# When ScalarE sums and squares an input tile, and where its shift comes from, in the shift-and-sign-convolution stage of a four-layer network

## The reference

```python
x = x + _L0_conv_ref(_gn(x), W, b, 224)   # mean over pixels @ W + b -> offsets (dy, dx), clipped to 0..28; gn(x) shifted by them
x = x + _L1_conv_ref(_gn(x), W, b)        # 3x3 convolution of sign(gn(x)) with the sum of four sign kernels, + bias
x = x + _L2_conv_ref(_gn(x), ...)         # DCT x FFT, mixing of 32 x 32 modes, inverse; + pointwise layer; relu
x = x + _L3_conv_ref(_gn(x), ...)         # the same with other weights
```

## Time and profile before

| | us |
|---|---|
| median of three runs | 3744.3 |
| the profiled execution | 3783.59 |
| its span (first to last instruction) | 3781.8 |
| PE busy | 3024.4 (80%) |
| DVE busy | 2752.2 (73%) |
| ACT busy | 1478.2 (39%) |
| first stage within it, roughly | 60 to 1893 |
| bodies 1 to 13 (first `add_conv` of body 1 to that of body 14) | 273 to 1730 |

### The profile page before, as it was taken

One profiled execution on the slowest core, in us unless ns is written; L12 is line 12 of the kernel. 1 busy time (PEld: TensorE's weight loads), 2 busy tenths in 40 slices (PEclk: granted clock), 3 DMA queues, 4 the chain that ended last, 5 costly groups with the idle time before them and its releaser, 6 DMA issues. The chain is left out here.

```text
span 3781.8 us, 58575 instructions
## 1 busy us (share of the span) xinstructions
PE 3024.4 (80%) x17264; PEld 1393.2 (37%) x17264; DVE 2752.2 (73%) x3864; ACT 1478.2 (39%) x2708; POOL 36.9 (1%) x23
## 2 busy tenths in 40 slices
PE   0288888888888888889937888989898835999997
PEld 0033334333334333344425333333333315444443
DVE  3887777787778687788342767676767644899998
ACT  3466666576666566664423322222222213000000
POOL 0000000000000000000010000000000010000000
PEclk9988888798888798889966999999898866999998
DMA  4676665666656566665274564646465353999998
GB/s 145 184 224 191 200 188 179 192 203 194 191 181 195 173 200 196 204 195 172 91 137 184 230 252 183 248 179 252 188 244 203 139 124 102 342 394 385 379 384 306
DMA packets 272195, 808.65 MB, mean 214 GB/s; under 512 B 85466, under 2 KB 119774, under 8 KB 261108
## 3 DMA queue, kind: packets, MB, share of 16 engines
q1 hardware_dynamic: 212948, 488.15, 40.9%
q10 hardware_dynamic: 58368, 316.72, 21.6%
q0 software_dynamic: 608, 0.63, 0.1%
HBM read 479.39 MB, written 329.56 MB: 214 GB/s over the span
## 5 line engine op out<-in xcount | busy, mean ns | idle before, releaser
L1397 ACT ACTIVATE B_junk<-B_im,B_nk 128x896 bf16<-128x896 f32 x224 | 232.7, 1039 | 749.3 <-DVE B_im L1455 610.4
L839 DVE SCALAR_TENSOR_TENSOR A_image<-A_cps,A_cbias,A_image 128x896 f32<-128x896 f32 x224 | 257.4, 1149 | 239.5 <-PE A_cps L470 239.1
L509 PE MATMUL A_vps<-A_tout,a_k_dctj 112*32 112x512 f32 x896 | 294.6, 792 | 150.6 <-ACT A_tout L614 150.6
L470 PE MATMUL A_cps<-A_sign,A_cfull 128*128 128x448 bf16 x1344 | 404.7, 384 | 7.7 <-issue 7.7
L1648 PE MATMUL C_ring<-C_im,C_wnorm 128*128 128x448 f32 x896 | 388.1, 572 | 23.7 <-DVE C_ubuf L1705 18.3
L1315 PE MATMUL B_ring<-B_rout,iB_k_rowf 128*64 128x512 f32 x896 | 306.6, 774 | 118.4 <-DVE B_rout L1448 118.4
L1343 PE MATMUL B_ring<-B_im,B_wnorm 128*128 128x448 f32 x896 | 384.9, 571 | 7.1 <-DVE B_wnorm L1426 4.9
L1455 DVE SCALAR_TENSOR_TENSOR B_im<-B_ring,B_im 128x896 f32<-128x896 f32 x224 | 239.0, 1084 | 183.9 <-PE B_ring L1353 182.3
L475 PE MATMUL A_cps<-A_sign,A_cedge 32*32 32x448 bf16 x1344 | 363.7, 379 | 0.0
L477 PE MATMUL A_cps<-A_sign,A_cedge 32*32 32x448 bf16 x1344 | 363.4, 378 | 0.0
L614 ACT ACTIVATE A_tout<-A_aps 112x512 f32<-112x512 f32 x448 | 246.1, 589 | 288.8 <-PE A_aps L498 288.3
(11 more groups left out here) (193 smaller groups left out, 3444.6 us busy)
## 6 DMA issues: line engine op xcount, KB each, us to landing
A_rin<-in_x SPq DMA_DIRECT2D x2016, 112.0 KB, 2.4
x2s<-A_image ACTq DMA_DIRECT2D x112, 896.0 KB, 4.6
B_im<-x2s SPq DMA_DIRECT2D x112, 896.0 KB, 9.7
x3s<-B_im ACTq DMA_DIRECT2D x112, 896.0 KB
C_im<-x3s SPq DMA_DIRECT2D x112, 896.0 KB, 11.9
out<-C_rout ACTq DMA_DIRECT2D x192, 256.0 KB
out<-C_rout ACTq DMA_DIRECT2D x192, 192.0 KB
out<-C_rout ACTq DMA_DIRECT2D x64, 128.0 KB
```

The source lines that it names most:

```text
L470: return nc.tensor.matmul(banks[:, s, 0:LPN], cfull[:, tap, :], lines(n, s, slice(0, P), 0, tap), start=(tap == 0), stop=(tap == 2), skip_ ...
L509: last = nc.tensor.matmul(vps[32 * g:32 * g + 32, :], con["k_dctj"][:, half, :], tout[G % OUTS][:, half, :], start=(half == 0), stop=(half ...
```

## The change

ACT's work on an input tile moves one slot later: `stat_tiles(s)` gives the load tiles of slot s - 1, and for each both sum and square are taken, in this order, with no lag between the two. `guess` no longer reads ACT's sum: DVE reduces the first 56 elements per partition of the image (part of tile 0) right after turning tile 0, waits for its own turn and its own reduce, and scales. In slot 14 ACT's `square` of output unit 13 comes ahead of `lower`. `PER` counts DVE's chained steps per body, one more now. The number of ACT instructions, of DMAs and of matmuls is the same.

```diff
-        def x_ops(k):
-            return [("sum", k)] + [("square", j) for j in {15: (13, 14, 15)}.get(k, (k - 2,)) if j >= 0]
+        def stat_tiles(s):
+            return x_tiles(s - 1) if s else range(0)
...
-                for k in x_tiles(s) if has_x else ():
-                    for op in x_ops(k):
-                        place[op] = len(place)
+                for k in stat_tiles(s) if has_x else ():
+                    for op in ("sum", "square"):
+                        place[op, k] = len(place)
...
             def x_tile(b, q, k, tile):
                 sum_x(b, q, k, tile)
-                if k >= 2:
-                    square_x(b, q, k - 2)
-                if k == TILES - 1:
-                    square_x(b, q, k - 1)
-                    square_x(b, q, k)
+                square_x(b, q, k)
...
+                    if has_v and 1 <= s <= UNITS:
+                        square(b, q, s - 1)
                     if has_x and s == 14:
                         lower(b + 1, (q + 2) % 3)
-                    if has_v and 1 <= s <= UNITS:
-                        square(b, q, s - 1)
                     if has_v and s in (5, 9, 13):
                         copy_rows(b, (s - 5) // 4)
-                    for k in x_tiles(s) if has_x else ():
+                    for k in stat_tiles(s) if has_x else ():
                         x_tile(b + 2, (q + 2) % 3, k, tile_no(b, x_at(k)))
...
-            def guess(b):
-                dve.wait_ge(junk_done, junk_x(b, ("sum", 0)) + 1)
-                nc.vector.tensor_scalar(nx[:], xsum[:, 0:1], -1.0 / TN, None, ALU.mult).then_inc(nx_ready, 1)
+            def guess(b, q):
+                dve.wait_ge(tile_turned, 1 if isinstance(b, int) and b == 0 else tile_no(b - 2, x_at(0)) + 1)
+                link(nc.vector.tensor_reduce(sm[:, 30:31], image[q][:, 0:2 * CHQ], AX.X, ALU.add))
+                nc.vector.tensor_scalar(nx[:], sm[:, 30:31], -0.5 / CHQ, None, ALU.mult).then_inc(nx_ready, 1)
...
-                if k == 2:
-                    guess(0)
+                if k == 0:
+                    guess(0, 0)
...
-                        if k == 2:
-                            guess(b + 2)
                         if k >= 8:
                             dve.wait_ge(junk_done, junk_x(b + 2, ("square", k - 8)) + 1)
                         turn_x(far, k, x_at(k) % RING, tile_loaded(b, x_at(k)))
+                        if k == 0:
+                            guess(b + 2, far)
...
-            PER = 41
+            PER = 42
```

## The result

The change makes the kernel slower: 3811.8 us in the median of four runs (3809.8 to 3820.3) against 3746.8 for the kernel before on the same chip, a ratio of 1.0145 (95% interval 1.0091 to 1.0199). I had forecast 3745. The ratios in this text are worked out from the single runs and aren't the quotients of the medians (that is 1.0173 here, or 65 us); by the ratio the loss is some 54 us. They leave out three runs in a slow state of the chip (one each of e1, e8 and the kernel before), which the medians hold.

What follows compares the result with a forecast made beforehand. Chains with waits, no full engine, were taken to bound the first stage. Points 1 to 4 summed as 0 + 0 + 0.8 + 0 = +0.8 us on 3744.3, giving 3745 us, range 3710 to 3774.

Steps and rivals of the forecast that it cites:

- What bounds it now: First stage: no engine full; chains with waits bound it, PE pacing slots 0 to 4, then DVE and SP's queue.
- Point 1, statistics one slot later: Slots 8 to 11: `copy_back` comes earlier, PE's idle time moves behind `forward_cols`; taken as 0, at most 50 us.
- The slower rival: Slot 11: PE's idle time now ends at unit 12's conv, at half clock; 3763 us, up to 3797; chance 0.33.
- no change: Whole kernel: the likeliest case, 3745 us, own range 3737 to 3752; chance 0.36.
- the clock has its own phase: Unit 12's conv: argument against all bodies turning slow, as the clock need not follow PE's gap; no size given.
- the 3 to 5 us that I had put down: Slot 11: forecast length of PE's idle time after `turn_back`, right up to DVE's sums.
- Point 2, the weight in even slots: ACT's statistics shift from odd to even slots, hidden behind other work; slot 2's 1.94 us wait stays; taken as 0.
- Points 3 and 4, the shift and the square: Shift in slot 0: +0.8 us in all; square first starts DVE's body 1.3 to 2.5 us sooner, swallowed: 0.
- The rival in which the earlier start counts: Body start: DVE's 1.3 to 2.5 us are not swallowed in slots 3 and 4; 3712 to 3727 us; chance 0.14.

Runs made afterwards that it cites:

- e1: The changed kernel with the old order, strips ahead of the output square; 3821.7 us, ratio 1.0158 against the kernel before.
- e8: The changed kernel with 34 unused matmuls on PE in slot 11, between `turn_back` and the averages; 3768.5 us, ratio 1.0055 against the kernel before.
- e7: The changed kernel with the first six stores of the output image issued one slot later; 3804.7 us, ratio 1.0161 against the kernel before.
- e10: The changed kernel with 28 unused matmuls on PE in slot 9, behind `forward_cols`; 3832.7 us, ratio 1.0153 against the kernel before.
- e2: The kernel before with only the output square put ahead of the strips; 3755.2 us, ratio 0.9998 against the kernel before.
- e3: The kernel before with only the shift taken from DVE's reduce behind the first turn; 3775.7 us, ratio 1.0040 against the kernel before.
- e9: The kernel before with 20 unused matmuls on PE ahead of slot 11's `forward_cols`; 3762.1 us, ratio 0.9987 against the kernel before.

## Why the prediction was wrong

*What bounds it now* held, but for a slip: 1451 us isn't the whole of bodies 1 to 13 (it is 1456.7, or 112.1 us a body instead of 111.6). DVE waits as before in slots 3 and 4; the rows of body 8 that answer to the earlier trace rows:

```profile
1124.14 1.15 DVE L836 SCALAR_TENSOR_TENSOR A_image<-A_cps,A_cbias,A_image 128x896 f32<-128x896 f32 x1 [4.22 <-PE A_cps L470]
...
1135.47 1.15 DVE L836 SCALAR_TENSOR_TENSOR A_image<-A_cps,A_cbias,A_image 128x896 f32<-128x896 f32 x1 [3.84 <-PE A_cps L470]
```

*Point 1, statistics one slot later: the step that failed.* Its 0 was wrong in two places, at the convs of units 12 and 13 (some 33 us with the slots behind them) and in the slots of the loads (13 us). For the first, its mechanism was told rightly, down to the sentence that the idle time "isn't removed but moved from ahead of `forward_cols` to behind it". Then it took 0 for it, because PE's idle time stays the same in sum. But idle time has two prices: its length, and the clock of what follows. Ahead of `forward_cols` the second price was paid by work with slack (3.63 us instead of 1.91); ahead of the averages it is paid by unit 12's conv, with DVE waiting for it. The trace of before held what was needed: 0.27 us of slack at the average said that `forward_cols` ended just in time, so taking its wait away could only open a gap there.

For the second, point 1 said that an earlier ACT is worth nothing "as long as DVE and SP set the pace there". They did, and what they wait for got worse: DVE's waits for loads rose from 78.2 to 95.3 us, and slots 6 to 10 by 1.0 us a body. That ACT also issues the stores, which go out earlier with the rest of its work, was no term of the sum; whether they are the reason is open but for e7.

*The slower rival* named this mechanism, place and the two kinds of body (1.10 and 3.73 us), and was ranked behind "no change". The size was off as well. It gave 18 us for unit 12, up to 34 more with unit 13. Measured: unit 12's waits grew by 46.0 - 34.8 = 11.2 us and unit 13's by 25.0 - 9.2 = 15.8, which is 27 of the 52 us in bodies 1 to 13. Slots 13 to 15 at a lower clock add 5 (0.4 a body); they come back in e8. Slots 6 to 10 add 13, which no rival named and which don't come back with the clock. The 0.5 us a body in slots 0 to 5 (6 us) is no more than the kernels differ by there (50.7 in the kernel after, 49.8 to 51.6 in those made from it). Body 0 is 6 us on top, in the same two places (3.5 us in its slots 11 and 12, 3.0 in slots 6 to 10). The gap was also longer than the 3 to 5 us that I had put down: 4.0 to 6.6. That was a slip of mine, since the terms that I named for it give 3.86 and half of 3.63 + 1.96, together 6.7; body 8 shows 6.58.

I had counted against this rival that "the clock has its own phase". Unit 13's wait does differ from body to body (0.7 to 3.3 us), but ahead of unit 12's conv PE idled 4.2 to 6.6 us in twelve of thirteen bodies, and the conv ran at half clock in all twelve. The rule that I cited (the Trainium skill, TensorE: Matmul & The Clock Gate, "HAM oscillation — how this bites in real kernels"), that a gap throttles PE and the work behind it starts cold, is borne out by e8, e10 and body 10.

*Point 2, the weight in even slots*, at 0: nothing speaks against it. The wait in slot 2 stayed to the hundredth, here in body 9, as the earlier trace rows:

```profile
1231.41 0.82 PE L498 MATMUL A_aps<-a_k_ident,A_image 128*112 128x128 f32 x4 [1.94 <-ACT A_colpart L628]
```

*Points 3 and 4, the shift and the square.* DVE and ACT from the end of body 8 into body 9, to be held against the earlier trace rows:

```profile
1209.18 1.11 DVE L803 STREAM_TRANSPOSE A_image<-A_rin 128x896 f32<-128x896 f32 x1 [0.78 <-DMA x2s<-A_image]
1210.33 0.21 DVE L742 TENSOR_REDUCE A_sm<-A_image 128x1 f32<-128x56 f32 x1
1210.58 0.15 DVE L743 TENSOR_SCALAR A_nx<-A_sm 128x1 f32<-128x1 f32 x1
```

```profile
1206.51 1.07 ACT L641 ACTIVATE A_junk<-A_image,A_nk 128x896 bf16<-128x896 f32 x1
1207.44 0.23 ACT L641 ACTIVATION_READ_ACCUMULATOR A_junk<-A_image,A_nk 128x1 f32 x1
1207.53 3.11 ACT L653 ACTIVATE A_image<-A_image,A_nbias 128x1792 f32<-128x1792 f32 x2
```

The square ends ahead of the strips, and the turn waits 0.78 us instead of 2.48, now for the store: 1.7 us sooner, inside my 1.3 to 2.5. The reduce takes 0.21 us (I took 0.2). Neither reaches the time, as e2 and e3 show, and as the prediction had it: the waits for PE in slots 3 and 4 swallow them. The rival in which the earlier start counts didn't come.

## What to carry to other kernels

Before you take away a wait of the matrix engine that costs nothing, look at what its idle time will stand in front of afterwards: ahead of work with slack a gap is cheap, ahead of the one conv that others wait for it cost 2.6 us each time. Look as well at what else the engine that becomes earlier will issue earlier: here stores, with 1.0 us a body of longer slots where loads are waited for. Where the order can be chosen, issue the large matmuls first and the small one that waits for another engine behind them. If the gap can't be moved, matmuls that nobody uses can fill it, but only if they reach to its end and not past it (20 were too few, 34 in some bodies too many).

## What the runs showed that I had not expected

The third layer, which is the same code in both kernels, ran in two lengths. Its stretch in the profiled executions of before and of after, in busy times (columns as in the earlier trace rows):

```profile
2048.00:3067.00 1019.00, 888.34 (x3968) 349.55 (x3968) 697.68 (x817) 248.92 (x448) 1.97 (x4) 0.90 0.53 210
```

```profile
2107.00:3093.00 986.00, 854.88 (x3968) 342.31 (x3968) 696.10 (x817) 248.90 (x448) 1.97 (x4) 0.94 0.54 217
```

The instruction counts are the same and the clock is not: 0.90 against 0.94, and 33 us. In the twelve experiments this layer took 986 to 995 us ten times and 1019 and 1021 in e2 and e10, one close to the kernel before and one close to the kernel after. What chooses between the lengths stays open. It may be part of why the runs of the kernel before spread over 3734 to 3794 us on the other chips, which wasn't tested. On record is that the spread goes with the clock: of the 25 runs on one chip the fastest (3735.3 us) had a mean granted clock of 0.892 and the slowest (3794.1) 0.876, with the others in between and not in two groups. It does show that one execution's time can't tell a change of 1% here, where the first stage alone could: its last `add_conv` came at 1877 to 1887 us in before, e2, e3 and e9, and at 1933 to 1940 in after, e1, e7 and e10.
